# The place of a transposition, of a low-rank product and of a difference in the hand-written order of a two-layer adaLN and LoRA kernel

## The reference, cut to what matters

```python
x = x + ffn0(cond0(x))     # cond0: grouped conv, 9 taps; ffn0: h @ W.T + b + (gated h @ A.T) @ B.T
x = x + ffn1(cond1(x))     # cond1: 64x64 mixing matrix per sample (8 kernels, softmax weights)
# ffn1: h @ W_base.T + b_base + sum_e sparsemax(h @ W_router.T + b)_e * (h @ lora_A[e]) @ lora_B[e]
```

## Time and profile before

| | |
|---|---|
| median of 3 runs | 504.34 us (503.76 to 504.69) |
| the profiled execution's own time | 504.13 us |
| its span, first to last instruction | 502.4 us |
| TensorE matmul busy | 496.9 us, 99% |
| VectorE busy | 360.0 us, 72% |
| ScalarE busy | 131.5 us, 26% |
| GpSimd busy | 143.3 us, 29% |
| granted TensorE clock, mean | 1.000 |

### The profile page before, as it was taken

One profiled execution on the slowest core, in us unless ns is written; L12 is line 12 of the kernel. 1 busy time (PEld: TensorE's weight loads), 2 busy tenths in 40 slices (PEclk: granted clock), 3 DMA queues, 4 the chain that ended last, 5 costly groups with the idle time before them and its releaser, 6 DMA issues.

```text
span 502.4 us, 8251 instructions
## 1 busy us (share of the span) xinstructions
PE 496.9 (99%) x2911; PEld 459.7 (92%) x2911; DVE 360.0 (72%) x828; ACT 131.5 (26%) x272; POOL 143.3 (29%) x122
## 2 busy tenths in 40 slices
PE   9999999999999999999999999999999999999997
PEld 8999999999999999999998888898998989899885
DVE  3966998857676787767898967786747567675753
ACT  4732344312333123331252321121212111111200
POOL 1000010003443133432205462451526235152620
PEclk9999999999999999999999999999999999999999
DMA  8844205428476475746999552334314243440212
GB/s 315 323 138 170 95 1 158 148 96 260 161 240 200 174 233 190 228 158 220 373 411 337 233 189 84 126 111 134 133 64 168 84 128 104 133 140 22 105 43 84
DMA packets 41124, 84.32 MB, mean 168 GB/s; under 512 B 3803, under 2 KB 16475, under 8 KB 41084
## 3 DMA queue, kind: packets, MB, share of 16 engines
q1 hardware_dynamic: 31884, 61.16, 36.2%
q10 hardware_dynamic: 9200, 22.65, 12.2%
HBM read 58.82 MB, written 24.97 MB: 167 GB/s over the span
## 4 chain that ended last, share of the span: by engine, by line
PE 85%; DVE 4%; issue 0%; ACT 0%; DVEq 0%
PE b_p L1321 10%; PE b_x L1339 7%; PE b_x L1342 7%; PE b_x L1341 7%; PE b_p L1322 5%; PE b_y L1341 5%; PE b_y L1342 5%; PE b_y L1339 5%; PE b_m L1287 4%; PE b_m L1297 3%; PE b_w L1339 2%; PE b_z L1341 2%; PE b_w L1341 2%; PE b_z L1339 2%; PE b_z L1342 2%; PE b_w L1342 2%
## 5 line engine op out<-in xcount | busy, mean ns | idle before, releaser
L583 ACT CAST a_hi<-mixed 128x512 fp32r<-128x512 f32 x63 | 38.1, 620 | 170.3 <-DVE mixed L895 90.4
L1321 PE MATMUL b_p<-wp,a_hi 128*128 128x464 f32 (+1 forms) x224 | 72.6, 377 | 0.0
L529 POOL TENSOR_TENSOR xs<-xs,mixw_sb 128x512 f32<-128x512 f32 x28 | 36.9, 1328 | 116.2 <-DMA xs<-x_scratch 86.8
L907 DVE TENSOR_TENSOR s_lo<-mixed,s_hi 128x512 fp32r<-128x512 f32 x56 | 46.0, 845 | 24.3 <-ACT s_hi L595 24.3
L1322 PE MATMUL b_p<-wp,a_lo 128*128 128x232 f32 (+1 forms) x224 | 60.1, 268 | 0.0
L595 ACT CAST s_hi<-mixed 128x512 fp32r<-128x512 f32 x56 | 34.7, 620 | 85.2 <-POOL mixed L501 49.4
L900 DVE TENSOR_TENSOR a_lo<-mixed,a_hi 128x512 fp32r<-128x512 f32 x63 | 50.4, 827 | 8.6 <-ACT a_hi L583 8.1
L501 POOL TENSOR_TENSOR mixed<-mixed 128x512 f32<-128x512 f32 x13 | 17.5, 1345 | 117.2 <-DVE a_lo L900 117.2
L1321 PEld LDWEIGHTS b_p<-wp,a_hi 128*128 128x128 f32 x224 | 42.0, 188 | 5.2
L1013 DVE TENSOR_TENSOR xs<-b_x,xs 128x464 f32<-128x464 f32 (+2 forms) x52 | 33.1, 637 | 16.4 <-PE b_x L1342 13.8
L1322 PEld LDWEIGHTS b_p<-wp,a_lo 128*128 128x128 f32 x224 | 42.7, 191 | 0.7
(11 more groups left out here) (263 smaller groups left out, 1193.7 us busy)
## 6 DMA issues: line engine op xcount, KB each, us to landing
blk<-x_scratch SPq DMA_DIRECT2D x16, 512.0 KB, 3.9
xs<-in_x SPq DMA_DIRECT2D x30, 256.0 KB, 3.1
x_scratch<-xs SPq DMA_DIRECT2D x30, 256.0 KB, 4.4
blk<-in_xblk SPq DMA_DIRECT2D x14, 516.0 KB, 4.3
xs<-x_scratch SPq DMA_DIRECT2D x28, 256.0 KB, 2.7
out_dram<-xs SPq DMA_DIRECT2D x28, 256.0 KB, 2.1
w_raw<-in_wcat SPq DMA_DIRECT2D x8, 546.0 KB, 8.6
praw<-in_wcat ACTq DMA_DIRECT2D x8, 464.0 KB, 5.8
```

Of the source, the lines that this page charges most:

```text
L529: pool.tensor_tensor(x_rows, x_rows, bbase[:, a:b], ALU.add).then_inc(x_biased[q], 1)
L583: act.copy(a_hi[:, op, :, :], mixed[:, op, :, :]).then_inc(ahi_done[op], 1)
L907: dve.tensor_tensor(s_lo[:, i, :, :], mixed[:, S_AT[i], :, :], hi(s_hi[:, i, :, :]), ALU.subtract).then_inc(slo_done[i], 1)
L1321: pe.matmul(both, x_hi, wp[:, k, :, 0:PLAIN[l]], start=(k == 0), stop=False, skip_group_check=True)
```

## The change

On TensorE, for pairs 8 to 14, turn_u(t2) moves from in front of P4 to behind it (pair 15 had it there). In the last pair, lora(t1) into b_z moves from in front of P6 to behind it. On VectorE, in the last pair, the addition of P6's bank moves in front of the one that takes b_z and of the left-over columns of the first tile. In pair 1, split_ut(2) moves in front of the last chunk's low parts of T2 and T4. No instruction is added or taken away.

```diff
@@ VectorE, pair 1
-            for kc in (2, 3):
-                for i in (T1, T2, T4):
-                    split_t(i, kc)
+            for i in (T1, T2, T4):
+                split_t(i, 2)
+            split_t(T1, 3)
             split_ut(2)
+            for i in (T2, T4):
+                split_t(i, 3)
             for kc in range(HK):
                 split_t(T3, kc)
@@ VectorE, every pair from FULL on
                 take(b_y, 3, g, took_p5)
+                if g == LAST:
+                    dve.wait_ge(p_done[P6], made(g))
+                    take(b_x, 1, g, took_u2)
                 dve.wait_ge(c11_done, g + 1)
                 dve.wait_ge(took_p1, made(g))
                 take(b_z, 0, g, fin11, BANK)
...
-                dve.wait_ge(p_done[P6], made(g))
-                take(b_x, 1, g, took_u2)
+                if g < LAST:
+                    dve.wait_ge(p_done[P6], made(g))
+                    take(b_x, 1, g, took_u2)
@@ TensorE
                     if together(t1):
                         turn_pair(g)
-                    else:
+                    elif g < PAIRS:
                         turn_u(t2)
...
                 product_a(g, P4, b_w, A22, T4)
-                if g == LAST:
+                if g >= PAIRS:
                     turn_u(t2)
...
                 product_s(g, P5, b_y, S1, T1)
                 if g == PAIRS:
                     pe.wait_ge(rank_lo, 2)
-                lora(t1, b_z, 0, BANK, c11_done)
-                if g < LAST:
+                if g < LAST:
+                    lora(t1, b_z, 0, BANK, c11_done)
                     mixture(t2 + 2, 0, b_m)
...
                     mixture(t2 + 2, 1, b_z)
+                else:
+                    lora(t1, b_z, 0, BANK, c11_done)
                 lora(t2, b_w, 0, BANK, c21_done)
```

## The result

The changed kernel takes 502.58 us (median of 13 runs, 502.02 to 503.61) against 504.34 us (13 runs): ratio 0.9966, 95% interval 0.9958 to 0.9974. That is 1.7 us less, with 1.3 to 2.1 in the interval. Forecast were 503.0 us and 1.33 us less, in a range of 502.2 to 504.1.

The account below looks back on a forecast made before the run. TensorE, busy 99%, was taken as the bound, so only its stalls could be gained: -0.44 - 0.59 - 0.30 = -1.33 on 504.13 gives 502.8; with the median 0.21 above that execution, 503.0 us, range 502.2 to 504.1.

Parts of the forecast that it names:

- Pair 1, -0.44: TensorE's low-rank matmul in pair 1: with VectorE's low part made earlier, the whole 0.44 us stall goes and stays gone.
- Pair 8, -0.02 out of 0.63: Pair 8's turn: of its 0.63 us stall only 0.02 is gained, the rest moves to P7, which waits for VectorE.
- Pair 9, -0.57: Pair 9's turn moved behind P4: its whole 0.57 us stall is gained, since VectorE has idle time there.
- Cost of the turn in its new place, 0: Turn behind P4 over seven pairs: the move itself taken as 0, bounded between +0.8 and -0.8 us.
- Last pair, -0.30: P7 of the last pair no longer held for took_u2, given the new orders on TensorE and VectorE: 0.30 us gained.
- Sum, -1.33: Whole kernel: -0.44 - 0.59 - 0.30 = -1.33 us on the profiled execution's 504.13.
- rival 1: Pair 8 gives its stall back too, VectorE's chain being partly led by TensorE: -1.94 us, 502.4; chance 0.08.
- Rival 2: Passage between the layers paced by transfers, pair 1's 0.44 waited away in pair 8: -0.89 us, 503.45; chance 0.20.

Follow-up runs that it names:

- t_pair8: Kernel before with the turn behind P4 in pair 8 alone; one trace, no timed run: 0.64 us won at the turn, 0.62 lost again by P7.
- a_up8: Changed kernel with pair 8's addition of P6's bank in front of B22's second half and the left-over columns: 502.67 us, ratio to before 0.9968.
- a_b22: Changed kernel with only the second half of B22's low part moved behind the addition of P6's bank in pair 8: 502.4 us, ratio to before 0.9963.
- a_pool8: Changed kernel with GpSimd's second to fourth bias additions of pair 8 held until VectorE's rank differences are done; one trace, offset to changed kernel -0.30 at the end.
- l_pe_only: Kernel before with only TensorE's half of the last pair's change, lora(t1) behind P6, VectorE's order as before: 505.65 us against 504.07, ratio 1.003.
- d_only_2: Second trace of the kernel before with only VectorE's order in pair 1 changed; that kernel was timed at 503.87 us against 504.34, ratio 0.9989.
- ctrl_before: Kernel before once more with no edit, a second trace: span 501.6 us instead of 502.4.
- ctrl_after: Changed kernel unchanged, its second trace, run again on the same chip as another variant: 502.69 us, ratio to before 0.9971.

## Why the prediction was right

- *Pair 1, -0.44*: measured 0.46 in three kernels, at the place and by the cause named. That it is kept to the end holds in both traces of the changed kernel. In the two traces of that part alone it was not, by stalls of pairs 3, 7 and 9 whose length followed the landing of a transfer.
- *Pair 8, -0.02 out of 0.63*: shown. t_pair8 gives 0.02. The path to it was a step longer than worked out: the forecast let TensorE reach P7 unheld at 288.25, but the mixture behind P6 waits for the same chain of VectorE and takes 0.18 of the 0.63 first. The sum stays, since P7 has the later wait. The cause is VectorE's chain, since freeing it by order (a_up8, a_b22) or by keeping GpSimd off it (a_pool8) frees P7. Had I stopped at the stall, I would have forecast 1.94.
- *Pair 9, -0.57*: 0.59 against the trace from which the forecast was made, 0.39 against the second one. The step was right for its trace, but the stall isn't a constant: it lay between 0.29 (l_pe_only) and 0.66 (d_only_2), with a mean of 0.46 over seven traces. The term was mis-sized by about 0.1, as it took one execution's load for all.
- *Cost of the turn in its new place, 0*: it is 0.02 to 0.03 cheaper per pair, 0.13 over pairs 10 to 14 and up to 0.18 over seven. The bounds around it (0.8 to either side) were far too wide, and the nearest row was right.
- *Last pair, -0.30*: 0.31 in the changed kernel, 0.30 alone. The need for VectorE's order was worked out ahead as a reason and is shown by l_pe_only. For the store of the first half tile the forecast names about 493 and, further down, near 492; it went out at 491.28, and nothing waited for it.
- *Sum, -1.33*: without start-up the traces of the changed kernel give 1.34 and 1.32 against ctrl_before, 1.52 and 1.50 against the first trace. The timed ratios give 1.7 (1.3 to 2.1) and, repeated, 1.5 (0.9 to 2.0). The forecast lies at the low edge of the first interval and inside the second. With the measured parts it would be 0.46 + 0.02 + 0.46 + 0.18 + 0.31 = 1.43: the cheaper turns, put at nothing, and pair 9's smaller mean stall partly cancel, which is luck. Whether the rest of the 1.7 is more than scatter stays open. The time alone would not have told the forecast from rival 1: its 1.94 lies in the interval too, and nearer to 1.7. Only the traces of pair 8 decide between them.

Rival 2 fell as put for the changed kernel (nothing was waited away in pair 8 by transfers), but its thought has some truth: d_only_2 came out just as this rival has it, 0.46 ahead in pair 1 and none of it left behind pair 9, and a_up8 shows that pair 9's start hangs on a store and a load that pair 8's left-over columns release. The forecast held against it that each transfer is issued on a signal and moves along. The issue does (16.3 us ahead of pair 9's mixture in all seven traces), but the time to landing differs, by 0.36 here and by 2 us for wp_place, and that is enough to take such a lead.

## What to carry to other kernels

When an engine is busy 99%, list its stalls one by one, and for each ask whether the releasing engine is itself waiting: if it has idle time behind the stall, the gain is kept; if it runs gapless up to the next place where it releases the first engine, the stall only moves there. The check is one subtraction at each such place behind it. A product moved on one queue and the additions that free its bank on another are one change: the half alone made this kernel 0.3% slower. And with gains near 0.1% each, compare stage by stage in traces, in more than one trace, since one program's spans differ by 0.8 us and a stall that ends on a load's landing had anything from 0.29 to 0.66.

## What the runs showed that I had not expected

The start-up, 7 us of loads and first products, differs between executions whatever the kernel: the first conditioning rows started at 7.05, 6.50 (the kernel before), 6.48, 6.78 (the changed one), and 6.40 to 7.30 in others, and ctrl_after fell another 0.5 behind up to 23 us. Two-input differences of VectorE beside GpSimd's cost more than their own time and depend on which starts first: 2.86 against 1.28 for the same two instructions, and 3.34 for two that take 1.3 alone, by the landing of a transfer. A held matmul cost 0.10 us over its wait wherever I read one: 0.31 or 0.32 to the next start instead of 0.21 (P7 in pair 8, in the last pair and in t_pair8), and 0.21 instead of 0.11 for the mixture of pair 8.
